# The feed-forward norm of layer 3 is made beside its graph convolution, the logit rows of layer 1 are split, and two W blocks of layer 0 get slots of their own

## The reference

```
for L in 0, 1, 2, 3:
    xn = layernorm(x)
    x  = x + gnn_L(xn, edges) + mix_L(xn)
    x  = x + ffn_L(layernorm(x))
L1 gnn:  h = xn @ W;  e = leaky_relu(al_s[src] + al_d[dst]) per head, softmax over the edges of a node, sum of h
L3 gnn:  out = A_norm @ (xn @ W) + b                       (graph convolution)
L3 mix:  y = xn' + attention(xn');  y + fc2(gelu(fc1(layernorm(y))))    (the norm and the MLP of the change)
L0 ffn:  a router picks 2 of 8 experts for each node
```

## Time and profile before

| | us |
|---|---|
| median of 3 runs | 3259.64 (3259.57 to 3264.41) |
| the profiled execution's own time | 3257.88 |
| its span in the profile | 3256.1 |
| PE busy | 3034.2 |
| DVE, POOL, ACT busy | 1715.0, 1427.5, 745.6 |

### The profile page before, as it was taken

How to read it: one execution, slowest core, us unless ns; L and a number is a source line. 1 busy time by engine, 2 the same in 40 slices (tenths; PEclk the granted TensorE clock), 3 DMA queues, 4 the chain that set the end, 5 groups by cost and what they waited for, 6 DMA issues and landing times.

```text
span 3256.1 us, 38168 instructions
## 1 busy us (share of the span) xinstructions
PE 3034.2 (93%) x13754; PEld 2351.7 (72%) x13754; DVE 1715.0 (53%) x2812; ACT 745.6 (23%) x1295; POOL 1427.5 (44%) x1007
## 2 busy tenths in 40 slices
PE   8999899999999996898998789899999998999988
PEld 3467577888888893676878358678888886877865
DVE  7734699475455536635775645543333336743132
ACT  1043211242333212102235221211111112212122
POOL 2022377524544451464540034456666664544620
PEclk9999999899999997998998899999999999999999
DMA  2011256212222121222210142123223332212313
GB/s 83 15 49 40 97 190 218 82 35 73 68 78 68 64 73 46 70 88 68 80 57 17 44 131 68 58 74 98 92 89 100 97 97 68 80 61 64 101 40 136
DMA packets 91283, 256.96 MB, mean 79 GB/s; under 512 B 10344, under 2 KB 10984, under 8 KB 90869
## 3 DMA queue, kind: packets, MB, share of 16 engines
q1 hardware_dynamic: 79488, 217.09, 20.8%
q10 hardware_dynamic: 11668, 38.19, 3.4%
HBM read 253.67 MB, written 1.57 MB: 78 GB/s over the span
## 4 chain that ended last, share of the span: by engine, by line
PE 85%; DVE 9%; issue 4%; ACT 2%; DMA 0%; ACTq 0%; DVEq 0%
PE ps L432 23%; PE ps L436 22%; PE ps L437 22%; PE ps L912 3%; DVE aux L2057 2%; PE ps L540 1%; PE ps L534 1%; PE ps L998 1%; PE ps L793 1%; PE ps L804 1%; PE ps L786 1%; PE ps L778 1%; DVE hot L2507 1%; DVE row L1867 1%; PE ps L613 1%
## 5 line engine op out<-in xcount | busy, mean ns | idle before, releaser
L367 POOL TENSOR_SCALAR w_hi<-raw 128x768 fp32r<-128x768 f32 x498 | 461.9, 927 | 1650.0 <-PE ps L432 1442.3
L370 POOL TENSOR_TENSOR w_lo<-raw,w_hi 128x768 fp32r<-128x768 f32 x498 | 974.2, 1956 | 41.5
L432 PE MATMUL ps<-H_hi,w_hi 128*128 128x512 f32 x804 | 320.1, 398 | 22.3 <-issue 11.6
L432 PE MATMUL ps<-A_hi,w_hi 128*128 128x512 f32 x780 | 309.4, 397 | 12.1 <-ACT scr L1630 12.1
L436 PE MATMUL ps<-H_lo,w_hi 128*128 128x512 f32 x804 | 316.9, 394 | 0.0
L437 PE MATMUL ps<-H_hi,w_lo 128*128 128x512 f32 x804 | 316.6, 394 | 0.0
L432 PE MATMUL ps<-B_hi,w_hi 128*128 128x512 f32 x720 | 292.0, 406 | 21.4 <-DVE B_lo L1851 15.2
L436 PE MATMUL ps<-A_lo,w_hi 128*128 128x512 f32 x780 | 305.8, 392 | 0.0
L437 PE MATMUL ps<-A_hi,w_lo 128*128 128x512 f32 x780 | 305.3, 391 | 0.0
L436 PE MATMUL ps<-B_lo,w_hi 128*128 128x512 f32 x720 | 283.6, 394 | 0.0
L437 PE MATMUL ps<-B_hi,w_lo 128*128 128x512 f32 x720 | 283.3, 393 | 0.0
(11 more groups left out here) (496 smaller groups left out, 5716.9 us busy)
## 6 DMA issues: line engine op xcount, KB each, us to landing
raw<-stream_dram SPq DMA_DIRECT2D x552, 384.0 KB, 3.0
w_ring<-w_dram ACTq DMA_DIRECT2D x45, 384.0 KB, 3.6
u_rows<-rows_dram ACTq DMA_DIRECT2D x8, 768.0 KB, 5.4
rows<-rows_dram ACTq DMA_DIRECT2D x7, 768.0 KB, 4.0
w_last<-w_dram ACTq DMA_DIRECT2D x9, 384.0 KB, 3.7
x<-x_dram ACTq DMA_DIRECT2D x1, 1536.0 KB, 8.9
out_dram<-x ACTq DMA_DIRECT2D x1, 1536.0 KB, 5.1
orf<-orf_dram ACTq DMA_DIRECT2D x6, 192.0 KB, 2.9
```

What stands on the lines that cost most here:

```text
L367: pool.tensor_scalar(w_hi[:, b // 3, b % 3], raw[:, b // 3, b % 3], 1.0, 1.0, ALU.mult, ALU.mult)\
L370: pool.tensor_tensor(w_lo[:, b // 3, b % 3], raw[:, b // 3, b % 3], w_hi[:, b // 3, b % 3], ALU.subtract)\
L432: mm = pe.matmul(o, wh, xh, start=first, stop=False, skip_group_check=True)
```

## The change

**Layer 0.** W blocks 4 and 5 go to two other buffers (`gat_w1`, in `head_f`) with semaphores of their own, and ACT loads them directly behind the norm. DVE makes blocks 0 to 2 inside `combine`, ahead of its wait for PE's transposes, and blocks 3 to 5 at the end of the first expert (before: 0 to 3 ahead of the first expert's work and 4, 5 at its end).

**Layer 1.** `gat_targets` makes a high and a low part of the terms in a new fp32r buffer `aux_r` (`gat_set`), and a logit row is two fp32r matmuls with a column of the identity, spread over 128 columns. The second half's terms come behind tile 0, head rows behind tiles 0, 1 and 3, and products 0 and 1 with rows 4 and 5 behind tiles 5 and 6. The engines' orders and the banks of tiles follow; DVE takes an inverse three heads late (before: two). The slope buffers alternate by head.

**Layer 3.** The norm of `acc` is made inside the feature turn: the sums behind its first half, the sums of squares behind the second and fourth tile of its second half. ACT casts node features straight from PSUM and DVE subtracts from PSUM and frees the bank. The scaled result goes to `A`, which the MLP reads. The additions to `x` (banks 0 to 5) come between the chunks of the norm from chunk 3 on (`between`), and the rest behind it.

```diff
-            def turn_n(X, reader, mid=None, since=None, last=True):
+            def turn_n(X, reader, mid=None, since=None, last=True, freed_by=None):
+
+                def tile_done(mm, b):
+                    done(mm, b, reader)
+                    S.pending[b] = freed_by or reader
...
-                    done(pe.matmul(ps[:, b], gat_sel[0:8, 4 * r + h % 4], aux[0:8, 2 + h // 4], start=True, stop=True), b, "act")
+                    pe.matmul(ps[:, b], ident_r[0:8, 4 * r + h % 4:4 * r + h % 4 + 1].to_broadcast([8, P]), gat_set[:, 2 + h // 4], start=True, stop=False)
+                    done(pe.matmul(ps[:, b], ident_r[0:8, 4 * r + h % 4:4 * r + h % 4 + 1].to_broadcast([8, P]), gat_set[:, h // 4], start=False, stop=True), b, "act")
...
-                    if t == 1:
+                    if t == 0:
                         gat_targets(1, 4)
-                    if t in (1, 2):
-                        gat_head_rows(t)
+                    if t in (0, 1, 3):
+                        gat_head_rows((1, 2, None, 3)[t])
+                    if t == 5:
+                        pe.wait_ge(act_to_pe, S.due(act_to_pe))
+                    if t in (5, 6):
+                        gat_product(t - 5)
+                        gat_head_rows(t - 1)
                 gat_features(beside_features)
-                gat_head_rows(3)
-                pe.wait_ge(act_to_pe, S.due(act_to_pe))
-                for h in range(GAT):
+                for h in range(2, GAT):
+                    if h == 4:
+                        pe.wait_ge(act_to_pe, S.due(act_to_pe))
                     gat_product(h)
-                    if h + 4 < GAT:
+                    if h < 4:
...
-                turn_n(A, "act", since=plain)
+                def sums_of_acc(g, m):
+                    if g == 0:
+                        for b in (4, 5, 6):
+                            use(b)
+                        for j in range(KC):
+                            mm = pe.matmul(ps[:, 6], ones[:, :], acc[:, j], start=j == 0, stop=j == KC - 1, skip_group_check=True)
+                        done(mm, 6, "dve")
+                    if g == 1 and m == 1:
+                        use(7)
+                    if g == 1 and m in (1, 3):
+                        for j in range(4) if m == 1 else range(4, KC):
+                            pe.wait_ge(act_to_pe, S.due(act_to_pe))
+                            mm = pe.matmul(ps[:, 7], ones[:, :], aux[:, j % 4], start=j == 0, stop=j == KC - 1,
+                                           skip_group_check=True)
+                            if j < 2:
+                                mm.then_inc(tile_for["act"], 1)
+                        if m == 3:
+                            done(mm, 7, "dve")
+
+                turn_n(A, "act", mid=sums_of_acc, since=plain, last=False, freed_by="dve")
                 graph_t("dve", True)
+                normed[:] = chunks_due()
             if part("mlp3"):
-                norm_of(acc)
-                gelu_mlp(B, "mlp3")
+                gelu_mlp(A, "mlp3")
...
-                act.dma_start(w1_ring[:, k % 4], t["w1"][GAT_W1 + k]).then_inc(w1_in[k % 4], 16)
+                act.dma_start(gat_w1(k), t["w1"][GAT_W1 + k])\
+                   .then_inc(w1_in[k] if k < 4 else gat_w1_in[k - 4], 16)
...
                 norm(x, acc, A)
+                for k in range(4, KC):
+                    load_gat_w1(k)
...
                 act.dma_start(sel[0:16, :], t["sel0"]).then_inc(sel_in, 16)
-                for k in range(4, KC):
-                    act.wait_ge(w1_free, GAT_W1 + k - 2)
-                    load_gat_w1(k)
...
-                for u in range(2 * NT):
-                    gat_feature(u)
-                    if u in (1, 2):
-                        gat_exps(u)
+                gat_feature(0)
+                gat_exps(1)
+                gat_feature(1)
+                gat_exps(2)
+                gat_feature(2)
+                gat_feature(3)
                 mark(act_to_pe)
                 gat_exps(3)
-                for h in range(4, GAT):
-                    gat_exps(h)
-                    gat_scaled(h - 4)
-                for h in range(GAT - 4, GAT):
+                gat_feature(4)
+                gat_feature(5)
+                gat_exps(4)
+                gat_feature(6)
+                gat_scaled(0)
+                gat_exps(5)
+                gat_feature(7)
+                mark(act_to_pe)
+                for h in range(1, 3):
+                    gat_scaled(h)
+                    gat_exps(h + 5)
+                for h in range(3, GAT):
...
-                features_n()
+
+                def nodes_of(g, tiles):
+                    for m in tiles:
+                        act.wait_ge(tile_for["act"], S.due(tile_for["act"]))
+                        act.copy(bn[:, m, 384 * g:384 * g + 384], ps[:, (4 * g + m) % 6, 0:384]).then_inc(act_to_dve, 1)
+
+                def squares(chunks):
+                    for j in chunks:
+                        act.wait_ge(dve_to_act, S.due(dve_to_act))
+                        if j >= 4:
+                            act.wait_ge(tile_for["act"], S.due(tile_for["act"]))
+                        act.activation(aux[:, j % 4], scr[:, j], ACT.Square).then_inc(act_to_pe, 1)
+
+                bn = B[0][:, :, :].rearrange("p k n -> p (k n)").rearrange("p (m d) -> p m d", m=NT)
+                nodes_of(0, range(NT))
+                squares(range(4))
+                nodes_of(1, range(2))
+                squares(range(4, KC))
+                nodes_of(1, range(2, NT))
+                act.wait_ge(dve_to_act, S.due(dve_to_act))
+                act.activation(row[:, :], row[:, :], ACT.Sqrt).then_inc(act_to_dve, 1)
+                for j in range(KC):
+                    act.wait_ge(dve_to_act, S.due(dve_to_act))
+                    act.activation(A[0][:, j], scr[:, j], ACT.Identity, bias=col("L3_mix_ln2_b", j)).then_inc(act_to_dve, 1)
             if "mlp3" in parts:
-                norm(acc, scr, B, "L3_mix_ln2_b")
...
+                    if between:
+                        between(j)
...
-                    dve.wait_ge(w1_in[k % 4], (w1_loads(k % 4) + k // 4 + 1) * 16)
+                    dve.wait_ge(w1_in[k] if k < 4 else gat_w1_in[k - 4], (w1_loads(k) + 1) * 16 if k < 4 else 16)
                     for r in range(2):
                         product = flat[:, r * D:r * D + D]
-                        S.step(dve.tensor_tensor(product, w1_ring[:, k % 4], rows[:, r], ALU.mult))
+                        S.step(dve.tensor_tensor(product, gat_w1(k), rows[:, r], ALU.mult))
...
-                freed(dve.tensor_copy(aux[0:8, 2 + half], ps[0:8, b]), b)
+                S.step(dve.tensor_copy(gat_set[:, 2 + half], ps[0:8, b]))
+                freed(dve.tensor_tensor(gat_set[:, half], ps[0:8, b], gat_set[:, 2 + half], ALU.subtract), b)
...
                    .then_inc(dve_to_pe, 1)
+                if beside:
+                    beside()
...
-                combine(8, gate_s[:, 6], gate_s[:, 10])
-                experts("experts0", 2, 10.0, True, lambda n: gat_vectors((range(4), range(4, KC))[n]) if n < 2 else None)
+                combine(8, gate_s[:, 6], gate_s[:, 10], lambda: gat_vectors(range(3)))
+                experts("experts0", 2, 10.0, True, lambda n: gat_vectors(range(3, KC)) if n == 1 else None)
...
-                    if h >= 2:
-                        gat_inverse(h - 2)
-                for h in range(GAT - 2, GAT):
+                    if h >= 3:
+                        gat_inverse(h - 3)
+                for h in range(GAT - 3, GAT):
...
-                features_n(marked=True)
-                add_t(x, "L3_gnn_b")
+                for g in range(2):
+                    for m in range(NT):
+                        c, b = slice(384 * g, 384 * g + 384), (4 * g + m) % 6
+                        dve.wait_ge(act_to_dve, S.due(act_to_dve))
+                        freed(dve.tensor_tensor(bn[1][:, m, c], ps[:, b, 0:384], bn[0][:, m, c], ALU.subtract), b)
+                    mark(dve_to_pe)
+                    if g == 0:
+                        centred(acc)
+                scaled(scr, A, 1e-8, "L3_mix_ln2_w", "L3_mix_ln2_b",
+                       lambda j: add_t(x, "L3_gnn_b", [j - 3]) if j >= 3 else None)
+                add_t(x, "L3_gnn_b", range(3, KC))
             if "mlp3" in parts:
-                norm(acc, scr, B, 1e-8, "L3_mix_ln2_w", "L3_mix_ln2_b")
                 gelu_mlp("mlp3", "L3_mix_fc2_b")
             if "ffn3" in parts:
                 def nodes_low():
```

More of the change, by code:

```diff
@@ L189, in build @@
         scr = sb("scr", [P, KC, N])
+        with ExitStack() as s:
+            aux_r = sb("aux_r", [P, 4, N], F32R, s)
         aux = sb("aux", [P, 4, N])
@@ L316, in build @@
         u_rows_in = [sem(f"u_rows_in{b}") for b in range(2)]
+        gat_w1_in = [sem(f"gat_w1_in{b}") for b in range(2)]
         w1_free, u_high, u_split = sem("w1_free"), sem("u_high"), sem("u_split")
@@ L494, in turn_n @@
```

(7 more changed lines are left out.)

23 lines of the change are left out of this document (14 added, 9 removed).

## The result

The changed kernel took 3227.51 us (median of 4 runs, 3223.88 to 3230.06) against 3261.04 (4 runs, 3259.57 to 3264.41) beside it: a ratio of 0.9898, interval 0.9883 to 0.9913. Forecast were 3225 us, range 3215 to 3237. The profiled execution took 3223.88 us for a span of 3222.1, that is 34.0 us less than the one before; the forecast of that difference was 34.3.

What follows compares the result with a forecast made beforehand. TensorE, busy 93% of the span, was taken to bound the kernel. Terms 11.7 + 12.6 + 10.0 = 34.3 us off 3257.9 gave 3223.6; with the runs' median 1.8 us above the profiled execution, 3225 us, range 3215 to 3237.

Steps and rivals of the forecast that it cites:

- Term 1: Layer 0, first expert: early loads and vectors remove most of PE's 12.10 us wait and its slow start; 11.7 us.
- hidden, with 4.9 us to spare: Layer 0: DVE's three blocks, 11.8 us, fit into its 16.72 us of idleness before the copies.
- Term 2: Layer 1, graph attention: split logit rows and the new order save PE work, waits and clock falls; 12.6 us.
- the 2.2 that I took off: Layer 1: two clock falls likely stay, behind the 2.7 us wait and before product 5; 2.2 us deducted.
- feature tiles stand between: Layer 1: argument against falls staying at the products, since feature tiles stand between and rows take half the time.
- Term 3: Layer 3: norm inside the feature turn removes 1.61 + 7.80 us of waiting and a slow start; 10.0 us.
- the one collision of 1.65 us: Layer 3's norm: one DVE subtraction slowed beside GpSimd eats the margin and costs 0.5; 1.0 us deducted for a bit over one.
- the margin: Layer 3: DVE frees bank 2 at 2929.5, 1.2 us before the graph convolution stops covering PE at 2930.7.
- The clock's falls at the products: Rival, layer 1: the clock still falls at the products; Term 2 is 5.6 us, kernel 3232; chance 0.17.
- The split rows were faster than fp32: Rival, layer 1, claimed the opposite: 8-partition fp32r rows no faster than fp32, 8 us lost, kernel 3234; chance 0.05.
- The other sign: Rival, layer 1: short row pairs keep PE's clock low through the whole attention stage; kernel 3286; chance 0.02.
- The 68.3 us that I held against it: Layer 1: a stretch said to hold four short row pairs has mean clock 0.88, so the clock does come back.

Runs made afterwards that it cites:

- the run without falls: The changed kernel with layer 1's head products 4 and 5 in banks 4 and 5 and four buffers for inverted sums: 3222.97 us, ratio 0.9886 to before.

## Why the prediction was right

The sum was 34.3 us and 34.0 came, but no term was exact: they missed by +1.4, -1.9 and +0.7 us, which all but cancel. The three mechanisms hold; that the total is right to 0.3 us is luck.

**Term 1**, 11.7 (10.2 to 12.5), came as 13.1, above its bounds. The wait gave 10.6 us (12.10 less 1.49) for 10.2. What was mis-sized was the clock: I left 0.8 us of a slow start to the remaining gap, and behind 1.49 us of waiting the clock was 1.00 for the next 5 us, so that the whole of it came back. A step that failed without a price was the cover: "hidden, with 4.9 us to spare" was 0.7, since I took a block at the 3.9 us that it took where GpSimd did not collide. Its timeline of the same stretch shows why, and the earlier trace rows had the price at hand.

**Term 2**, 12.6 (5.6 to 14.8), came as 10.7. PE's work was 65.1 us and not 61.4, as the run without falls shows: a pair of rows 1.12 us for 0.91, since the step into the first of them and out of the last costs 0.33 and 0.32 us; a feature tile 3.2 for 3.12, a product 3.65 for 3.57. The waits were 4.5 us for 8.7: the wait for the second terms was 2.03 us at full clock in the run without falls and 0.45 in the changed kernel, whose tile 0 ran partly at half clock, so that fall cost nothing. The falls cost 5.1 for the 2.2 that I took off. I had placed them behind the wait for the terms and ahead of product 5; they came in tile 0 and in product 4. The step "feature tiles stand between" the rows was not the reason that the others went: the old order with short rows loses no more.

**Term 3**, 10.0 (7.2 to 11.0), came as 10.7. The late one was the third addition to `x`, by 0.72 us where I took off 1.0; two scalings and a low part lost 2.9 us to GpSimd, more than the one collision of 1.65 us that I reckoned with, but the margin was 2.2 us and not 1.2. Waits and slow start make 10.3 us; what the other 0.4 are is open.

**The rivals.** The clock's falls at the products did not stay: in the changed kernel one was left, behind a wait. The split rows were faster than fp32, by 0.8 us a pair. The other sign was nowhere near: the clock over the stage is 0.93, above the 0.88 of before. The 68.3 us that I held against it contain all eight pairs of rows, not four, which makes that argument stronger.

**The rules.** The Trainium skill (TensorE: Matmul & The Clock Gate, "Why this matters for your kernels") ties falls to idle gaps between bursts. With split rows the runs agree in part: every fall in a product stood behind a gap, but longer gaps between two products brought none, and the falls in the first feature tile had no gap ahead of them. With fp32 rows they don't agree: the clock fell in four products in a row with no wait ahead of them. The Trainium skill (SBUF — State Buffer, "SBUF: two separate sides") has VectorE and GpSimd share a pair of ports under an exclusive lock, held for a whole instruction. Holding GpSimd's blocks back took the slowness away entirely (0.75 us for 2.32), which agrees, and applied to layer 0 the rule would have corrected term 1's cover.

What stays open is why the clock falls with fp32 rows at four places in one order and six in the other, why a first fall in tile 0 comes in some traces only, and why 2.3 us between two products are followed by a fall with fp32 rows and by none with split ones. No run here tells it.

## What to carry to other kernels

Before work is moved into an idle stretch, read what GpSimd does in that stretch: a VectorE operation with two SBUF operands beside a subtraction of GpSimd took 2.4 us for 0.96, and cover shrinks by it. Where a long wait has one engine named as its end, ask who would have ended it otherwise, since undoing one of two equal causes gave nothing. A low stretch of the clock may hide in waits, and waits in it: here a stage took 74.4 us with 3.4 us of low clock and with 10.2, and two free PSUM banks took away 3.0 us of waits together with 1.7 of clock.

## What the runs showed of the hardware

- An fp32r matmul of 512 columns with 8 partitions took 0.23 us from start to start, like one with 128 partitions, and a change to or from other matmuls 0.33 and 0.32. The fp32 rows show two records for each matmul, 0.48 us apart (1.91 for the four of a pair).
- Behind a wait of 1.49 to 1.53 us ahead of long matmuls the clock stayed at 1.00 in nine kernels, and fell behind one of 1.78. Between split 8-partition rows and 98-column products one of 1.14 to 1.22 us was followed by 3.4 to 7 us at half clock in eight kernels of eight, while 0.93 to 2.29 us between two such products was followed by none; with fp32 rows 2.28 us there was.
- With fp32 rows the clock fell for 3.4 us in each of four products (5.44 us for 3.65) with PE busy throughout.
- The slowing goes both ways: in layer 0's stretch GpSimd's `w_hi` took 1.54 us, where the earlier trace rows have 0.83 and 0.85 with VectorE idle or on PSUM.
